# An 8-head graph attention layer as a four-stage pipeline over groups, and 4-head layers whose weights and maximum lie in PSUM

## What is computed

```python
# layer 0: 8 heads of 32, edge features
h = (x @ W.T).reshape(n, 8, 32); h_src, h_dst = h[src], h[dst]
alpha = sum(h_src * a_src) + sum(h_dst * a_dst)
enc = relu(edge_attr @ edge_W.T + edge_b).reshape(-1, 8, 32)
alpha = alpha + sum(enc * h_dst);  alpha = where(alpha >= 0, alpha, 0.2 * alpha)
ex = exp(alpha - segment_max(alpha, dst)[dst])
out = segment_sum(h_src * (ex / segment_sum(ex, dst)[dst])[..., None], dst) + bias
# layers 1 to 3: mean of x[src] by dst, two linear maps, relu between
# layer 4: normalised sum of (x W)[src] by dst, relu
# layers 5, 6: 4 heads of 64; alpha = leaky_relu(el[src] + er[dst]), softmax by dst, residual, elu
# layernorm(x + ...) after layers 0, 3, 4 and 6
```

## Time and profile before

| | us |
|---|---|
| median of 3 runs | 7030.29 (7014.93 to 7047.85) |
| the profiled execution's own time | 7030.79 |
| its span | 7028.9 |
| layer 0, from its first gathers to its last add | 1655 |
| TensorE busy (matmul) | 3578.5 |
| GpSimd busy | 3308.5 |
| VectorE busy | 2252.4 |
| ScalarE busy | 1015.1 |

### The profile page before, as it was taken

How to read it: one execution, slowest core, us unless ns; L and a number is a source line. 1 busy time by engine, 2 the same in 40 slices (tenths; PEclk the granted TensorE clock), 3 DMA queues, 4 the chain that set the end, 5 groups by cost and what they waited for, 6 DMA issues and landing times.

```text
span 7028.9 us, 66855 instructions
## 1 busy us (share of the span) xinstructions
PE 3578.5 (51%) x16350; PEld 2607.2 (37%) x16351; DVE 2252.4 (32%) x6651; ACT 1015.1 (14%) x2763; POOL 3308.5 (47%) x3409
## 2 busy tenths in 40 slices
PE   4545455445644454445444463445466665455555
PEld 3434344344433343333333342333344443344443
DVE  2434444444311121111111231111244445344444
ACT  1111111111200000000100010000122222222222
POOL 3444444544056645664466506664255551555540
PEclk7656566566667677677777766766666666666675
DMA  3222222222023222322222203222243331433330
GB/s 111 70 70 70 76 72 73 76 65 61 15 83 87 84 67 85 86 85 70 82 87 85 73 15 88 85 86 60 69 107 105 106 105 52 118 105 104 105 87 19
DMA packets 332933, 553.52 MB, mean 79 GB/s; under 512 B 175666, under 2 KB 211562, under 8 KB 332306
## 3 DMA queue, kind: packets, MB, share of 16 engines
q0 software_dynamic: 160384, 449.20, 22.5%
q1 hardware_dynamic: 172386, 102.66, 5.3%
HBM read 521.42 MB, written 30.20 MB: 78 GB/s over the span
## 4 chain that ended last, share of the span: by engine, by line
another core or an unknown queue 36%; PE 28%; issue 18%; DVE 12%; ACT 2%; DVEq 2%; POOL 1%; DMA 0%; SPq 0%; ACTq 0%; POOLq 0%
PE ps L414 7%; PE ps L577 6%; PE ps L701 2%; PE ps L404 2%; PE ps L688 2%; DVE rows L1057 2%; PE ps L666 1%; PE ps L672 1%; PE ps L421 1%; DVE segmax L1046 1%; DVE rows L905 1%; PE ps L650 1%; PE ps L470 1%; PE ps L678 1%
## 5 line engine op out<-in xcount | busy, mean ns | idle before, releaser
L1377 POOL DMA_INDIRECT rows<-table,src_idx x2912 | 2889.7, 992 | 2421.6 <-issue 874.5
L414 PE MATMUL ps<-rows,attr 128*128 128x256 f32 x3328 | 1037.3, 480 | 230.7 <-issue 141.6
L414 PEld LDWEIGHTS ps<-rows,attr 128*128 128x128 f32 x3328 | 804.4, 248 | 447.1 <-issue 286.4
L1367 POOL DMA_INDIRECT drows<-table,dst_idx x416 | 394.5, 948 | 801.3 <-DVEq L929 607.2
L421 PE MATMUL ps<-ident,rows 128*128 128x128 f32 x416 | 117.4, 375 | 1239.3 <-ACT rows L775 869.1
L842 DVE TENSOR_TENSOR acc<-acc,ps 128x256 f32 x260 | 108.6, 418 | 1993.1 <-PE ps L421 1179.6
L421 PEld LDWEIGHTS ps<-ident,rows 128*128 128x128 f32 x416 | 51.1, 172 | 1322.6 <-ACT rows L775 923.6
L775 ACT ACTIVATE rows<-ps 128x256 f32<-128x256 f32 x208 | 79.7, 383 | 2541.3 <-remote 1769.5
L833 DVE TENSOR_SCALAR attr<-iota,local 128x128 f32<-128x128 f32 x1664 | 352.9, 299 | 207.7 <-issue 191.6
L495 PE MATMUL ps<-ident,shifted 64*128 64x64 f32 x52 | 17.5, 336 | 698.2 <-issue 362.0
L577 PE MATMUL ps<-rows,attr 128*128 128x260 f32 x832 | 331.5, 553 | 34.8 <-DVE rows L1057 33.9
(11 more groups left out here) (213 smaller groups left out, 4939.5 us busy)
## 6 DMA issues: line engine op xcount, KB each, us to landing
drows<-in_tiles SPq DMA_DIRECT2D x104, 512.0 KB
rows<-table,src_idx POOLq DMA_INDIRECT x2912
table<-rows SPq DMA_DIRECT2D x20, 640.0 KB, 3.3
drows<-table,dst_idx POOLq DMA_INDIRECT x416
table<-rows SPq DMA_DIRECT2D x10, 660.0 KB, 3.4
pens<-pen_rows SPq DMA_DIRECT2D x104, 48.1 KB
table<-rows SPq DMA_DIRECT2D x5, 680.0 KB, 3.4
gat_pen_row<-pen_ends SPq DMA_DIRECT2D x208, 0.1 KB
```

The lines of the kernel that those rows point to most:

```text
L414: ins = mm(node_ps[par % 2], sum_hot[:, par % 2, k, :], src_rows(l, par)[:, k, 0:D], start=k == 0, stop=k == T - 1)
L1367: pool.indirect_dma_start(drows[:, k // 4, k % 4, :], None, tables[l][:, :], bass.IndirectOffsetOnAxis(ap=dst_idx[:, g * T + k:g * T + k + ...
L1377: pool.indirect_dma_start(src_rows(l, par)[:, k, :], None, tables[l][:, :], bass.IndirectOffsetOnAxis(ap=src_idx[:, g * T + k:g * T + k + ...
```

## The change

Layer 0 is written anew in the manner of layers 5 and 6, with one more stage. In step g the engines work on four groups: the sums and messages of g, the maximum and weights of g+1, the encoding and destination part of the scores of g+2 (in quarters of two tiles), and the one-hot of g+3. All layers now have 4 row buffers.

- The gathers by destination go. For each tile SyncE loads `spans`, the 128 table rows from the tile's first destination on (a plain DMA at an address that it reads from `tile_base`), and TensorE multiplies them by a one-hot (`edge_turned`) into `h_ps`: `spread`. The row of destinations (now bf16) is loaded by `high_of`, one group ahead of the spans.
- The columns of table 0 are reordered to 8 source scores, then 8 blocks of 33: the head's destination score and its 32 features. `enc` has a 1 in the score's place, so that one product and one sum give both parts. The encoding is a bf16 product over 36 rows: attributes and weights are split in three bf16 parts each at the start, and written to DRAM in all nine pairings. ScalarE makes the relu (`encoded`).
- The weights lie in the rows' first 8 columns with a 1 behind them, so that the sums give the denominators and the degree too. The messages are made in place, in two halves.
- The penalties come from `pen_rows` as in layers 5 and 6, `dseg` and `marks` go.
- In both kinds of layer the carry's edge row is one more row of the permutation matrix, which takes two products out of `edges`.
- Layers 5 and 6: the weights are written twice, to the rows and to PSUM (`gat_ex_ps`), and the messages read those in PSUM; the running maximum lies in PSUM (`gat_max_ps`); the rescale factor is read from PSUM without a copy; `near` is turned once a layer by TensorE into `near_all` in SBUF, and a group's part is copied by ScalarE instead of loaded.

The core of the diff follows (`maxima`, `carry`, `scans`, `add_group` of layer 0 are those of `gat_dve` with 8 heads; of the three steps the tests on n = g + 1 and m = g + 2, for the layer's ends, are cut). First the buffers and TensorE:

```diff
-ROW_BUFS = [2 if k[0] == "gat_edge" else SUM_BUFS for k in LAYERS]
+ROW_BUFS = [SUM_BUFS] * NL
...
+            def encode(m, j, h, q):
+                par, turn = pair_of(j, h)
+                if q == 0:
+                    pe.wait_ge(attr_landed[par], 16 * (turn + 1))
+                if not (q == 0 and isinstance(m, int) and m == 0):
+                    pe.wait_ge(enc_copied, 4 * m + q)
+                for i in range(2):
+                    k = 2 * q + i
+                    ins = mm(enc_ps[:, i, :], attr[:, par, k * P:(k + 1) * P], w_enc[:, :], start=True, stop=True)
+                ins.then_inc(enc_ready, 1)
+
+            def spread(m, j, h, q):
+                par, turn = pair_of(j, h)
+                if q == 0:
+                    pe.wait_ge(edge_turned_ready, m + 1)
+                pe.wait_ge(span_landed[q], 32 * (m + 1))
+                if not (q == 0 and isinstance(m, int) and m == 0):
+                    pe.wait_ge(prod_ready, 4 * m + q)
+                for i in range(2):
+                    k = 2 * q + i
+                    ins = mm(ps[:, i, 0:TW], edge_turned[:, par, k, :], spans[:, k, :], start=True, stop=True)
+                ins.then_inc(h_ready, 1)
...
+            def step(g, h, j):
+                    encode(*of_m, 0)
+                    spread(*of_m, 0)
+                    encode(*of_m, 1)
+                sums(g, j, 0, range(0, 4))
+                    turn_scores(n)
+                    spread(*of_m, 1)
+                    encode(*of_m, 2)
+                    edges(n)
+                    spread(*of_m, 2)
+                    encode(*of_m, 3)
+                    carries(n)
+                sums(g, j, 1, range(4, 6))
+                sum_tiles(j % 2, j, range(6, 8)).then_inc(node_ready, 1)
+                    spread(*of_m, 3)
+                    turn_back(n)
+                turn_sums(g, j)
+                    rescales(n, j + 1)
```

VectorE in layer 0:

```diff
+            def products(m, q):
+                at = 4 * m + q
+                dve.wait_ge(enc_copied, at + 1)
+                dve.wait_ge(h_ready, at + 1)
+                V.tensor_tensor(prod[:, q % 2, :, :], enc[:, q % 2, :, :], h_ps[:, :, H:TW], ALU.mult).then_inc(prod_ready, 1)
...
+            def step(g, h, j):
+                messages(g, j, 0)
+                    turned_hots(m + 1, *of_x)
+                    add_group(g - 1, (j - 1) % 2)
+                    products(m, 0)
+                    edge_scores(n, *of_n)
+                messages(g, j, 1)
+                    reductions(m, 0)
+                    scans(n, *of_n)
+                    products(m, 1)
+                    carry(n, of_n[0] % 2)
+                    reductions(m, 1)
+                    products(m, 2)
+                    maxima(n, of_n[0] % 2)
+                    reductions(m, 2)
+                rescale_node(g, j % 2)
+                    products(m, 3)
+                    reductions(m, 3)
```

SyncE's loads for group x of layer 0:

```diff
+            def edge_tables(x, h, par):
+                early = isinstance(x, int) and x < 2
...
+                elif not is_last(x):
+                    sp.wait_ge(edge_turned_ready, x)
+                    high_of(x + 1, 1 - par)
+                if not early:
+                    sp.wait_ge(enc_ready, 4 * x - 4)
+                sp.dma_start(attr[:, par, :], attr_parts[:, bass.ds(x * T * P, T * P)]).then_inc(attr_landed[par], 16)
+                for q in range(4):
+                    if not (early and x == 0):
+                        sp.wait_ge(h_ready, 4 * x + q - 3)
+                    for k in (2 * q, 2 * q + 1):
+                        node = sp.value_load(tile_base[0:1, bass.ds(x * T + k, 1)], min_val=0, max_val=NPAD - P)
+                        sp.dma_start(spans[:, k, :], tables[0][bass.ds(node, P), :]).then_inc(span_landed[q], 16)
+                sp.wait_ge(seg_free, x + 1)
...
```

The weights, the messages and the maximum of layers 5 and 6:

```diff
+                nc.scalar.activation(gat_ex_ps[b % 2], exponents, ACT.Exp)
+                nc.scalar.activation(src_rows(l, b)[:, :, D:D + H], exponents, ACT.Exp).then_inc(ex_ready, 1)
...
-                                x[:, :, D:D + H].unsqueeze(3).broadcast_to([P, 4, H, D // H]), ALU.mult).then_inc(msg_ready, 1)
+                                gat_ex_ps[b % 2][:, 4 * half:4 * half + 4, :].unsqueeze(3).broadcast_to([P, 4, H, D // H]), ALU.mult).then_inc(msg_ready, 1)
...
-                ch.then(V.tensor_tensor(segmax[0:TH, :], fwd[0:TH, :], bwd[0:TH, :], ALU.max))
+                ch.then(V.tensor_tensor(gat_max_ps, fwd[0:TH, :], bwd[0:TH, :], ALU.max))
```

More of the change, by code:

```diff
@@ new lines, in step @@
+            def step(g, h, j):
+                n = None if is_last(g) else g + 1
+                m = None if n is None or is_last(n) else n + 1
+                b = (j + 1) % SUM_BUFS
+                if m is not None:
+                    encoded(m, 0)
+                    encoded(m, 1)
+                if n is not None:
+                    hot(n, b % 2, 0)
+                if m is not None:
+                    encoded(m, 2)
+                if n is not None:
+                    hot(n, b % 2, 1)
+                if m is not None:
+                    encoded(m, 3)
+                node_sums_out(g, j)
+                if n is not None:
+                    weights(n, b)
+                    rescales(n, b)
@@ L734, in gat_act @@
+            act.wait_ge(aside, ASIDE)
+            nc.scalar.activation(enc.rearrange("p b t (h d) -> p (b t h) d", h=H)[:, :, 0:1], unit[:, :].unsqueeze(2).broadcast_to([P, 4 * H, 1]), ACT.Copy)
+            for q in range(4):
+                encoded(0, q)
+            hot(0, 0, 0)
+            hot(0, 0, 1)
+            for q in range(4):
+                encoded(1, q)
+            weights(0, 0)
+            rescales(0, 0)
+            gat_loop(act, step)
         def gat_act(act, l):
@@ new lines, in edge_dve @@
+            edge_row = edge_perm[TH:TH + 1, :, :, :]
+            V.memset(fwd[TH:TH + 1, :], 1.0)
+            V.memset(bwd[TH:TH + 1, :], 1.0)
+            ch.then(V.memset(edge_row, 0.0))
+            ch.then(V.memset(edge_row[:, 0, :, 0:1], -BIG))
+            ch.then(V.memset(edge_row[:, 1, :, T:SLOTS], -BIG))
+            turned_hots(0, 0, 0)
+            for q in range(4):
+                products(0, q)
+                reductions(0, q)
+            turned_hots(1, 1, 0)
+            turned_hots(2, 2, 0)
@@ new lines, in edge_dve, with sum_dve, make_onehot, add_window @@
+            products(1, 0)
+            edge_scores(0, 0, 0)
+            reductions(1, 0)
+            scans(0, 0, 0)
+            products(1, 1)
+            carry(0, 0)
+            reductions(1, 1)
+            products(1, 2)
+            maxima(0, 0)
+            reductions(1, 2)
+            products(1, 3)
+            reductions(1, 3)
+            ch.flat()
+            stepping(dve, ch, step, EDGE_STEPS)
+            add_group(NG - 1, 1)
+        def sum_dve(dve, l, turns, sum_turns):
+            V = nc.vector
+            node_reg = dve.alloc_register(f"node{l}")
+            def make_onehot(g, k, w, par):
+                return V.tensor_scalar(sum_hot[:, par % 2, k, :], iota[:, 0:P] if w is None else iota[:, bass.ds(w * P, P)],
+                                       local[:, bass.ds(g * T + k, 1)], None, ALU.is_equal)
+            def add_window(node, par):
+                win = acc[:, :, bass.ds(node, P)]
+                return V.tensor_tensor(win, win, sums_ps[par % 2], ALU.add)
+            def add_group(g, par):
@@ L999, in gat_dve @@
+            hot_group(0, 0)
+            sum_loop(dve, step)
         def gat_dve(dve, l, ch, turns, sum_turns):
```

859 lines of the change are left out of this document (467 added, 392 removed).

## The result

The changed kernel takes 6363.1 us (median of 4 runs, 6351.5 to 6375.4) beside 7033.4 (4 runs) of the kernel before on the same chip: ratio 0.9057, 95% interval 0.9026 to 0.9088. The forecast was 6367. The profiled execution took 6351.5 us, its span is 6349.5, the mean granted clock 0.71 against 0.672. That the total came within 4 us is luck: the two large misses inside the forecast, 66 us in the 8-head layer and 56 in the 4-head layers, nearly cancelled.

The account below looks back on a forecast made before the run. Bound: a ring of VectorE's add, a batch of gathers and TensorE's late signals. 7028.9 - 570 (8-head layer) - 114 (4-head layers) + 20 (start) = 6364.9 us for the span, 6367 for the kernel; range 6080 to 6700.

Parts of the forecast that it names:

- The ring: 8-head layer: VectorE's add, a batch of 8 gathers, TensorE's late signals and VectorE's way to the next add bound it; 18.2 us.
- The fourth spread: 8-head layer: the last quarter's spread, two tiles at 0.83 us, comes on top of 18.2 us, giving 19.9, say 20.0.
- the quarters: Rival, 17%: in the 8-head layer the four spread quarters serialise between TensorE and VectorE; 25.7 us a group, 6663 in all.
- The fill: Start of the 8-head layer: GpSimd starts with 32 gathers while SyncE loads the first spans; 45 us, once.
- The layer: The whole 8-head layer: 52 groups x 20.0 us + 45 = 1085 us, -570 us.
- SyncE: 8-head layer: SyncE issues 13 DMAs a group instead of 3, 13.1 us, under the step, with no one waiting for it.
- the order in its queue: 8-head layer: SyncE issues the broadcast row ahead of the spans; worth 0 by itself, a step later if it came last.
- The 4-head layers: Message weights read from PSUM end the first gather's slowdown, 2.01 to 0.95 us; 104 x 1.1 = -114 us, bounds 0 and -200.
- the fixed 1.2 us to the late signals: In the ring, TensorE's signals, held back during a batch of gathers, were taken to arrive 1.2 us after it ends.
- The start: Before the layers: attributes split in three bf16 parts, written nine times, ahead of the first table store; +20 us, bounds +5 and +45.
- Turning `near`: Turning `near` by small products in place of its way through DRAM: 0.
- The rival that the late signals go: Rival, 20%: with 8 gathers over a longer 8-head step signals aren't late; VectorE bounds it, 14.5 us a group, kernel 6081 us.

## Why the forecast held

**The ring.** Right. Cutting the batch and taking gathers out shorten the step, lightening SyncE hardly does. Over some 42 full batches of the 8-head layer it is, by means, 0.6 us from the add to the first gather, 10.2 of batch and 8.4 from its end to the next add, 19.2 (by medians 0.3, 10.0, 6.9); I had 1.0 + 11.4 + 7.5. The batch was mis-sized: I gave its first gather 2.01 us, as the messages keep two SBUF inputs, but it mostly starts outside them (0.95 by median; the second one at 603.18 does meet L1063, 1.80). The tail was too short (8.4 for 7.5) and took some of it back.

**The fourth spread, the quarters.** The rival of 25.7 us did not come: TensorE's work was 14.6 us a group, not 18.4: the 16 tiles of sums and spread took (251.0 + 273.5) / 47 = 11.2 for 13.4, at a clock of 0.79 where I had read their price at 0.68. VectorE (12.0 for 13.1) and the encoding (85.9 / 374 = 0.23 us a tile for 0.25) were near. The 1.7 us that the fourth spread was to put on top of the ring were never taken out by themselves, so that term stays unshown. Groups of instructions of the changed kernel, 200 to 1100 (busy, mean ns, idle before):

```profile
L489 PE MATMUL ps<-rows,rT 128*128 128x272 f32 x752 | 273.5, 523 | 16.6 <-DVE rows L1063 16.6
L454 PE MATMUL ps<-rT,attr 128*128 128x272 f32 x748 | 251.0, 465 | 34.6 <-issue 17.0 <-DVE norm L1009 16.2 <-DMA rT<-table 1.4
...
L441 PE MATMUL ps<-w_enc,norm 36*128 36x256 bf16 x374 | 85.9, 317 | 6.1 <-issue 5.2 <-ACT rT L818 0.4
```


**The fill.** 45.2 us from first gather to first scores (105.2 to 150.4), forecast 45. **The layer:** -636 with its node pass for -570. It took 1028.9 us (105.2 to 1134.1) for the 1085 forecast, and 52 x 1.04 = 54 of those 56 are the step. The other 10 of the 66 are a misread start: the 1655 us before were counted from 100, but the first gathers begin at 90.7, so the layer took 1664.6.

**SyncE.** 13 DMAs, nobody waiting: right. That it would be busy "over half" of the step was too small, it never stops; and the order in its queue, the row ahead of the spans, is worth 94 us, not 0, because of it.

**The 4-head layers.** Mechanism right and shown by undoing it; size wrong, -58 for -114: the failed term is the fixed 1.2 us to the late signals.

**The start** +14.5 for +20. **Turning `near`** was put at 0; the fill of the first 4-head layer grew by 6.7 us and that of the second by 0.9, and whether the turning is the cause was not tried.

**The rival that the late signals go** (step 14.5, for 20%) did not come in the first measurement and is the case on another chip, at 14.01 us. I had tied it to the number of gathers alone; the same 8 gathers a group are late on one chip and not on another. Its bound was not the one I named either: at 14.01 VectorE is busy for 509.43 / 600 of the step, 11.9 us, and TensorE for 12.4.

VectorE's L1242 starts 0.48 us after L620's end there and 4.69 in the first trace. Why is open: the instructions are the same, and nothing in either trace names the cause. No chip on record shows both behaviours and none was run again later, so that it is the chip, and not its state at the time, is not shown. One difference lies in the traces beside the waits: the first holds fewer records of signals than instructions that give them, of all engines (150 for the 208 of VectorE's L1009, 142 for the 208 of ScalarE's L818), the other nearly all (207 and all). So signals in general, and not TensorE's alone, or even their recording, may be what differs; no run tells these apart.

## What to carry to other kernels

Weigh a step against the whole loop that closes it: a term cut from a batch of gathers comes back as far as the next link is tied to the batch's start rather than to its end. On a queue that is never idle the order of issue is worth microseconds a step, though no one seems to wait for the queue. Before tuning against a wait that no instruction explains, run the kernel on a second chip: cutting the batches won 3.4% on one (6131 us, 0.8751 for 0.9057), and another form of the cut, with pauses, lost 4.4% on another; none is shown here to beat the changed kernel on both. And where a backlog is suspected, count the pauses as well as the batches.

## What the hardware showed beyond expectation

- The same kernel took 6363 us on one chip and 5065 on another, the kernel before 7033 and 5502, and of the 1266 us between the changed kernel's two spans some 1210 lie in the steps, whose "remote" waits are the main difference the traces show: sum layers 12.4 against 10.05 us a group, 4-head 15.0 against 10.3, 8-head 18.96 against 14.01.
- Where signals are late, they are late with 6 gathers in a row and hardly ever (one wait of 3.1 us in over 100 batches) with 4 that stand over 3 us behind another 4. In the 4-head layers, behind a pause of under 2 us, 28 batches of four out of 33 had a late signal. Eight gathers hold the signal of L620 until 12.0 us after their start. In the same stretch SyncE's two DMAs of L1536 took 3.11 us for 1.42.
- TensorE's granted clock in the 8-head layer was 0.79 with these waits (busy for 694 of 900 us), 0.93 without (533 of 600) and 0.61 in the old kernel (819 of 1655).
